# Storing and reloading the quarter sums from ScalarE's queue, with the orders of all engines written anew

## The reference, cut to what matters

```python
# x: (64, 12, 224, 224) f32
pooled = x.reshape(64, 12, 14, 16, 14, 16).sum(axis=(3, 5))
h = einsum('bcij,ce->bije', pooled, channel_weights).reshape(64, 196, 192)
# attention, 12 heads, causal, over the 196 tokens of layernorm(h);
# only the ceil(sqrt(196)) = 14 tokens with the largest selection weight get it
h = h + attention(layernorm(h))
h = h + gelu(layernorm(h) @ in_weight.T + in_bias) @ out_weight   # hidden 768
```

## Time and profile before

| what | us |
|---|---|
| median of 3 runs (lowest, highest) | 908.95 (907.29, 917.83) |
| the profiled execution, whole | 907.97 |
| its span in the trace | 906.3 |
| PE busy in the span | 619.0 (68%) |
| PE weight loads busy | 508.9 (56%) |
| DVE busy | 529.9 (58%) |
| ACT busy | 335.3 (37%) |
| POOL busy | 156.6 (17%) |

### The profile page before, as it was taken

The page is one execution under the profiler, slowest core; times in us unless marked ns, Lnnn a source line. Parts: engine busy times, 40 slices in busy tenths (PEclk is TensorE's granted clock), DMA queues, the critical chain, the costliest instruction groups (busy, mean ns, idle before and its releaser), DMA issues.

```text
span 906.3 us, 12215 instructions
## 1 busy us (share of the span) xinstructions
PE 619.0 (68%) x3860; PEld 508.9 (56%) x3860; DVE 529.9 (58%) x1357; ACT 335.3 (37%) x826; POOL 156.6 (17%) x212
## 2 busy tenths in 40 slices
PE   0373278484949499494976848685794849499996
PEld 0161156373837377373955637474673738387875
DVE  0958457393829538393664927376482938387322
ACT  0002126161716225171542606253361616164651
POOL 1103021121222012121212112120221211211100
PEclk9985559696978859697797958888796969789999
DMA  9995939597686938768394965859396886740000
GB/s 307 323 276 139 301 68 279 161 270 197 169 270 159 280 84 229 214 177 263 76 335 110 296 151 147 287 121 317 92 298 150 250 217 157 252 89 14 31 28 31
DMA packets 66380, 172.55 MB, mean 190 GB/s; under 512 B 4456, under 2 KB 56872, under 8 KB 60170
## 3 DMA queue, kind: packets, MB, share of 16 engines
q1 hardware_dynamic: 35840, 114.93, 34.4%
q0 software_dynamic: 26112, 44.73, 28.7%
q10 hardware_dynamic: 4362, 12.07, 4.1%
HBM read 158.99 MB, written 12.73 MB: 189 GB/s over the span
## 4 chain that ended last, share of the span: by engine, by line
DMA 29%; PE 27%; DVE 20%; issue 16%; POOL 4%; ACT 1%; ACTq 1%; SPq 1%; POOLq 0%; DVEq 0%
DMA patch_sums<-R 15%; DVE R L884 14%; DMA X<-in_x 8%; PE psO L597 8%; DMA OB<-in_ob 4%; PE psS L536 4%; PE psS L521 3%; DMA Praw<-patch_sums 2%; PE psF L585 2%; PE psC L572 2%; DVE Sm L1006 2%; DVE mx L1010 2%; PE psA L474 2%; POOL X L351 1%; PE psS L548 1%
## 5 line engine op out<-in xcount | busy, mean ns | idle before, releaser
L597 PE MATMUL psO<-W,act 128*112 128x192 f32 x1344 | 285.8, 354 | 0.6 <-ACT obuf L728 0.6
L884 DVE TENSOR_REDUCE R<-X 128x42 f32<-128x1344 f32 (+1 forms) x112 | 234.8, 2140 | 31.5 <-DMA X<-in_x 31.4
L597 PEld LDWEIGHTS psO<-W,act 128*112 128x112 f32 x1344 | 234.4, 192 | 23.5 <-issue 16.8
L721 ACT ACTIVATE act<-psF 128x392 f32<-128x392 f32 x192 | 95.6, 498 | 313.1 <-PE psF L585 313.0
L474 PE MATMUL psA<-TMR,P 49*98 49x108 f32 x64 | 16.1, 403 | 177.5 <-POOL P L367 175.5
L474 PEld LDWEIGHTS psA<-TMR,P 49*98 49x98 f32 x64 | 11.8, 266 | 181.9 <-POOL P L367 179.1
L351 POOL DMA_DIRECT2D X<-in_x x64 | 84.2, 1421 | 153.8 <-DMA X<-in_x 150.6
L910 DVE COPY F<-psA 98x216 f32<-98x216 f32 x16 | 6.1, 380 | 178.9 <-PE psA L474 178.9
L585 PE MATMUL psF<-Stk,M1S 104*128 104x392 bf16 x192 | 72.4, 377 | 5.4 <-ACT act L721 5.3
L360 POOL TENSOR_TENSOR Pt<-Praw 48x196 f32<-48x196 f32 x16 | 8.6, 536 | 256.2 <-DMA Praw<-patch_sums 256.2
L728 ACT ACTIVATE obuf<-psO 112x192 f32<-112x192 f32 x112 | 35.8, 320 | 35.2 <-PE psO L601 35.2
(11 more groups left out here) (190 smaller groups left out, 925.2 us busy)
## 6 DMA issues: line engine op xcount, KB each, us to landing
X<-in_x SPq DMA_DIRECT2D x48, 1344.0 KB, 12.7
X<-in_x SPq DMA_DIRECT2D x64, 672.0 KB, 13.5
X<-in_x POOLq DMA_DIRECT2D x64, 672.0 KB, 12.5
out<-obuf ACTq DMA_DIRECT2D x16, 588.0 KB, 3.5
patch_sums<-R SPq DMA_DIRECT2D x16, 147.0 KB, 17.4
Praw<-patch_sums SPq DMA_DIRECT2D x16, 147.0 KB, 2.6
W1T<-in_w1t ACTq DMA_DIRECT2D x1, 576.0 KB
W<-in_w ACTq DMA_DIRECT2D x1, 576.0 KB
```

The source lines that it names most:

```text
L597: pe.matmul(to, act_sb[u % 2][:, m, i * OT:(i + 1) * OT], W2[:, m, :], start=(m == 0), stop=False)
L721: act.activation(act_sb[u % 2][:, n // 2, (n % 2) * (GT // 2):(n % 2 + 1) * (GT // 2)], psF[:, 0:GT // 2], ACT.Gelu).then_inc(act_F1.sem, 1)
L884: dve.tensor_reduce(R[:, r, t * TQ * N:(t + 1) * TQ * N].rearrange("p (q j) -> p q j", q=TQ), v, AX.XY, ALU.add).then_inc(dve_L, 1)
```

## The change

The store of the quarter sums and its reload leave SP's round and become two entries of ScalarE's plan, `R:st:0` and `R:ld:0`. They are the same two DMAs with the same waits, now on the queue that also carries the outputs. SP issues x loads only. The plans of all engines but SP are replaced by new ones; no computation is added or removed.

```diff
@@ SyncE
-                g, r = 4 * i + k - 1, (k - 1) % 2
+                g = 4 * i + k - 1
...
-                if active(g):
-                    sp.wait_ge(dve_L, XT * g + XT)
-                    sp.dma_start(scratch[bass.ds(g, 1)].rearrange("o p q -> (o p) q"), R[:, r, :]).then_inc(sums_out[r], 16)
-                    sp.wait_ge(sums_out[r], landed(g, r))
-                    if exists(g - 2):
-                        sp.wait_ge(pool_P.sem, pool_P.at(g - 2, "q23"))
-                    sp.dma_start(Praw[:, r, :], sums_in[bass.ds(g, 1)].rearrange("o p q -> (o p) q")).then_inc(sums_back[r], 16)
@@ ScalarE
+            def step_R(g, u, name):
+                r = u % 2
+                if name == "st":
+                    act.wait_ge(dve_L, XT * g + XT)
+                    act.dma_start(scratch[bass.ds(g, 1)].rearrange("o p q -> (o p) q"), R[:, r, :]).then_inc(sums_out[r], 16)
+                else:
+                    act.wait_ge(sums_out[r], landed(g, r))
+                    if exists(g - 2):
+                        act.wait_ge(pool_P.sem, pool_P.at(g - 2, "q23"))
+                    act.dma_start(Praw[:, r, :], sums_in[bass.ds(g, 1)].rearrange("o p q -> (o p) q")).then_inc(sums_back[r], 16)
...
@@ GpSimd's plan
-            plan = ("X:2:1 P:s:2 X:4:1 K:v:2 K:d1:2 K:d2:2 X:6:1 X:0:0 c:s:4").split()
+            plan = ("K:v:2 K:d1:2 X:6:1 K:d2:2 X:0:0 X:2:0 P:s:1 X:4:0 c:s:4").split()
```

More of the change, by code:

```diff
@@ L601, in step_F2 @@
                     pe.matmul(to, Stk2[u % 2][:, i * OT:(i + 1) * OT], RS[:, :], start=False, stop=True).then_inc(pe_F2.sem, 1)
-            plan = ("K:tr2:1 f:0:1 o:3.2:2 S:g:2 o:4.0:2 f:1:1 A:sl:1 o:4.1:2 f:2:1 at:0:2 at:1:2 at:2:2 f:3:1 "
-                    "o:4.2:2 f:4:1 A:st:1 o:5.0:2 f:5:1 o:5.1:2 G:ga:1 f:6:1 o:5.2:2 f:7:1 A:tm:0 o:6.0:2 C:xt:2 "
-                    "f:8:1 o:6.1:2 f:9:1 G:u:1 C:fa:2 f:10:1 o:6.2:2 f:11:1 A:zt:0 S:sc:1 o:0.0:1 o:0.1:1 o:0.2:1 "
-                    "o:1.0:1 o:1.1:1 o:1.2:1 o:2.0:1 o:2.1:1 C:fb:2 o:2.2:1 o:3.0:1 o:3.1:1 K:tr1:0 C:f2:2 S:et:1").split()
+            plan = ("o:2.0:2 o:2.1:2 o:2.2:2 o:3.0:2 o:3.1:2 o:3.2:2 K:tr1:1 S:et:2 o:4.0:2 f:0:1 K:tr2:1 o:4.1:2 "
+                    "S:g:2 A:sl:1 f:1:1 o:4.2:2 f:2:1 at:0:2 f:3:1 at:1:2 at:2:2 f:4:1 o:5.0:2 A:st:1 o:5.1:2 f:5:1 "
+                    "G:ga:1 f:6:1 o:5.2:2 G:u:1 f:7:1 A:tm:0 o:6.0:2 f:8:1 C:xt:2 o:6.1:2 f:9:1 C:fa:2 S:sc:1 f:10:1 "
+                    "o:6.2:2 f:11:1 A:zt:0 C:fb:2 o:0.0:1 o:0.1:1 o:0.2:1 C:f2:2 o:1.0:1 o:1.1:1 o:1.2:1").split()
             def body(i, k):
@@ L732, in step_F2 @@
                                   obuf[u % 2][:, :, :].rearrange("p i e -> p (i e)")).then_inc(y_out[u % 2], 16)
-            plan = ("S:t:2 K:k2:1 f:0:1 f:1:1 O:3:2 f:2:1 f:3:1 f:4:1 f:5:1 O:4:2 f:6:1 f:7:1 O:5:2 C:XH:2 f:8:1 "
-                    "f:9:1 f:10:1 G:rs:1 f:11:1 A:fm:0 C:ga:2 A:e:0 K:H:0 O:6:2 O:0:1 K:M:0 S:e0:1 S:e1:1 S:e2:1 "
-                    "S:e3:1 S:e4:1 S:e5:1 O:1:1 K:L:0 C:gb:2 S:n:1 O:2:1 K:k1:0").split()
+            plan = ("S:e0:2 S:e1:2 O:0:2 S:e2:2 S:e3:2 S:e4:2 K:H:1 S:e5:2 O:1:2 K:M:1 S:n:2 K:L:1 O:2:2 K:k1:1 "
+                    "S:t:2 K:k2:1 f:0:1 f:1:1 f:2:1 R:st:0 f:3:1 O:3:2 R:ld:0 O:4:2 f:4:1 f:5:1 f:6:1 O:5:2 f:7:1 "
+                    "G:rs:1 f:8:1 C:XH:2 f:9:1 C:ga:2 f:10:1 O:6:2 A:fm:0 f:11:1 C:gb:2 A:e:0").split()
             def body(i, k):
@@ L751, in body @@
                     else:
-                        {"A": step_A, "G": step_G, "K": step_K, "S": step_S}[stage](g, u, step)
+                        {"A": step_A, "G": step_G, "K": step_K, "R": step_R, "S": step_S}[stage](g, u, step)
             weights()
@@ L1068, in prepare @@
                         weights_heads(m)
-            plan = ("C:os:4 A:sel:2 S:g:3 A:top:2 S:at:3 A:slots:2 C:xh:3 L:0:0 G:ga:2 A:var:1 A:log:1 G:u:2 "
-                    "A:var2:1 S:sc:2 L:1:0 L:2:0 S:ri:2 L:3:0 L:4:0 L:5:0 L:6:0").split()
+            plan = ("S:g:3 A:top:2 C:os:4 S:at:3 A:slots:2 G:ga:2 C:xh:3 L:0:0 G:u:2 A:var:1 A:log:1 S:sc:2 A:var2:1 "
+                    "L:1:0 S:ri:2 L:2:0 L:3:0 A:sel:1 L:4:0 L:5:0 L:6:0").split()
             def body(i, k):
```

## The result

The changed kernel takes **826.01 us** (median of 4 runs, 823.70 to 831.32) against 911.05 (907.29 to 917.83) for the kernel before: a ratio of 0.9067, 95% interval 0.8995 to 0.9139. The forecast was 729, range 695 to 790. The direction was right and the size was not: 85 us came instead of 180, and the time lies outside the range.

What follows compares the result with a forecast made beforehand. The store queued behind x on SP was taken to bound the kernel. Summed: 64 to first store, intervals of 36 and 42, 13 x 38.4 = 499, end 85: span 726, median 729 us; range 695 to 790.

Steps and rivals of the forecast that it cites:

- What bounds the kernel before: Store of the sums queues behind x loads on SP, landing in 17.6 us; 49.1 us turn, no full engine.
- Nothing is passed: Rival: store on ScalarE's queue still waits for x, landing in 14 to 16.5 us; 909 us; chance 0.04.
- The price of store and reload: On ScalarE's queue, priced by packets plus unloaded time: store 5.0 us, reload 3.5 us.
- X:2 ahead of P costs nothing: GpSimd's add of tile 2 precedes P; its tile lands before P is due, so cost is nothing.
- Tokens to mask: Queries before P shorten TensorE's path: scores 2.9 us after tokens, 4.7 with C steps, against 7.7 before.
- above 0.95: Expected sign: TensorE's granted clock above 0.95, with its wait for P 3 us or less.
- Mask to store: VectorE's stretch to the last sum gains var2, 2.9 us, and small A:sel instructions, 0.6; scores to last sum 21.9.
- Cost nil: ScalarE stands about 2 us at the reload; TensorE has other work meanwhile, so no cost unless landing is late.
- The sum and the rest: Interval 38.4 us, 13 of them 499; start 64, first two intervals 36 and 42, end 85; span 726.
- The 1.1 us of allowance: Added per interval for waits the sum leaves out, such as x halves landing late; raises 37.3 to 38.4 us.
- x becomes the bound: Rival: x loads and adds fill the DMA engines, 42.5 us per interval, 785 us; chance 0.20 including other waits.
- The DVE waits for x in most rounds: Sign of being wrong: VectorE waiting for x in most rounds; no size given.

Runs made afterwards that it cites:

- e1: Kernel before with only store and reload moved to ScalarE's queue, all other orders kept; 825.03 us median of four, 814.0 from the two runs compared.
- e2: Changed kernel with its new orders, but store and reload back on SyncE; 907.5 us, ratio 0.9972.
- e7: Changed kernel storing 64 of 128 rows and reloading 16 of 48 from the third group on; 801.38 us, one run.
- e16: e15 with GpSimd's add of tile 2 issued behind P; 749.58 us, ratio 0.8205.
- e13: e11 with SyncE also waiting for the store's landing before loading tile 3, so tiles 3 and 4 start later; 764.66 us.
- e4: Changed kernel with GpSimd's add of tile 2 issued behind P instead of before; 806.86 us, ratio 0.8864.
- e15: Changed kernel with tiles 5 and 6 loaded after the reload's landing and the reload two places later in ScalarE's order; 795.94 us.
- e6: Changed kernel with only a third of each x tile loaded and added from the second group on; 676.03 us, one run.
- e3: Changed kernel with var2, VectorE's second-layernorm chain, put back ahead of the scores' step; 815.51 us, ratio 0.8958.
- e12: Changed kernel with var2 ahead of the scores' step, tile 2's add behind P, and the reload two places later on ScalarE; 800.91 us.
- e5: Changed kernel without GpSimd's adds, so two sevenths of x are never read; 781.11 us, one run.
- e10: Changed kernel, var2 before scores' step, tile 2's add behind P, tiles 5 and 6 after reload's landing; 777.46 us median, 766.9 from two compared.
- e11: e10 with the reload two places later in ScalarE's order, behind O:4 and Gelu f:4; 751.02 us, ratio 0.8209.

## Why the prediction was wrong where it was

**What bounds the kernel before: right.** The store stood behind x in SP's queue. e1 moves nothing but the queue and has the whole gain; e2 moves everything else and has none. "Nothing is passed" fell: store 17.4 to 6.8 us. The Trainium skill ("DMA: Bandwidth & Descriptors", section "Issuing engines are not separate DMA queues") says that several issuing engines only save the issuing time; here the issuing engine was worth 85 us, through the queue ahead of the store. The same section says that DMAs of different engines interleave, and with that the traces agree: the store got through in 6.8 us while x was moving.

**The price of store and reload: the step that failed.** The forecast read 2.6 packets per us and DMA engine off ScalarE's queue from 10 to 20 us and charged 8 and 3 packets, 5.0 and 3.5 us. Measured, with the 0.35 around them: 6.97 and 7.32 us for 5.2 and 3.65, so 5.4 of the 7.56 us by which the interval missed. The row was a throughput with many packets queued; a lone small transfer pays something else. It is 4.6 us for each of the two in the changed kernel (2.5 to 2.9 for the reload beside x or an add alone), shrinks far less than the transfer (e7: 3.9 at half a store, 3.0 at a third of a reload) and goes away when x loads and adds aren't beside it (e16 for the reload, e13 for the store). Why a small transfer costs that under load stays open. The forecast had the reload with the smaller surcharge, for its fewer packets; it got the larger.

**"X:2 ahead of P costs nothing": wrong.** I looked for lateness of GpSimd and found none, rightly; but the same entry puts 672 KB beside the reload. e4: 19 us; with x held, e15 to e16: 46 us.

**Tokens to mask: 6.1 forecast, 7.99 measured.** The order of work was right (e6: 5.95). TensorE's wait for P is what was forecast, 3 us or less (41.8 us in 15 places, 2.8 each). The forecast took a wait so short to cost no clock (above 0.95); it does: the mean is 0.86, in 12 of 13 intervals TensorE went part or all of the way from tokens to scores at the lower level, and in 3 of them the scores themselves did, 4.26 us for 2.24.

**Mask to store: 20.5 forecast, 21.86 measured.** var2 stands there as forecast; the rest is VectorE waiting for x (1.6 us per interval) and for exponentials (0.5; 1.80 at 263.76). The forecast had 1.1 us for all such waits. Moving var2 out brought 10 us in e3 and none between e16 and e11.

**"Cost nil" of ScalarE's waits: wrong in kind.** Forecast 2 us at the reload; measured 50.2 us in 12 places, 4.2 each, as the landing is later. In the changed kernel that costs little (e12: none); it is what holds TensorE once the reload is quick (e5; e10 to e11: 16 us).

**The sum and the rest.** Interval 45.96 - 38.4 = 7.56, times 13 = 98 us; the third store at 138.33 for 142: -3.7; the end 86.2 for 85: +1.2. Together 96, from 726 to the span of 822.0. The 1.1 us of allowance were not enough for the terms above. The DMA engines' share over the 13 intervals is 0.81, where above 0.9 was forecast. The rival "x becomes the bound" is refuted at its number: it asked 42.5 us per interval of x itself, and e11 and e16 move all of x in 40.70. But its subject was right: x mostly slows the round trip of the sums, and it is waited for as well, in 10 of 13 intervals. "The DVE waits for x in most rounds" was one of the prediction's own signs of being wrong, and it came true; with 1.6 us per interval it is the smaller part. e16, three small moves on the changed kernel, recovers 76 of the 97 us between forecast and result; its interval of 40.70 still has 1.6 us more in store, reload and tokens, 0.4 to the mask and 1.4 behind it than the forecast's 37.3.

The range was too narrow for the same reason: the store's 6.8 us lie within the 8 that it allowed, but for the reload, which took 7.0, it allowed nothing above 3.5.

## What to carry to other kernels

A small transfer on the critical path should be priced from a small transfer that ran beside the traffic that it will have, not from the throughput of a queue; and the traffic beside it is set by whoever issues at that moment, so look at what the order of the other engines' DMAs puts there, even where it makes no engine late. Moving a store to a queue without big loads is the first half of the gain; keeping big loads and an add away from its reload, and waiting for its landing a little later, was nearly the second here (826 to 750 us). Held back from the store as well, the loads met the reload, and the time rose (e13). After each such step look at who waits next: an engine that waits for a landing holds all that stands behind it, and that only shows once the landing's successor is quick.
